# Attention as a rotation lane and a score lane with banks of their own, rotation from PSUM, one global projection run, head products in two column halves

## What is computed

```python
x = L0_attn_x                       # (16, 512, 128)
xn = _layernorm(x)
s = _L0_attn_ref(xn, ...)           # gated linear recurrence ("gru"), 256 states
g = _silu(_L0_ffn_ref(xn, ...))     # two layers: windowed attention + gated MLP
x = x + s * g
xn = _layernorm(x)
s = _L1_attn_ref(xn, ...)           # softmax attention, 16 heads ("glob")
g = _silu(_L1_ffn_ref(xn, ...))     # 8 experts, top 2
x = x + s * g

# one layer of _L0_ffn_ref
q, k, v = split(shift_token(x) @ wqkv, 3)          # 8 heads of 64
q, k = rotary_xpos(l2norm(q) * qs, l2norm(k) * ksc)
x = x + local_attention(q, k, v) @ wo              # windows of 64 and the one before
h = layernorm(shift_token(x)) @ w1 + b1
x = x + (a * gelu(g)) @ w2 + b2                    # a, g = split(h, 2)

# _L1_attn_ref
sim = einsum('bnkh,bmhk->bnhm', q, k)              # keys of 16, values of 64
attn = softmax(sim * scale, axis=1)                # over n
o = einsum('bnhm,bmhv->bnhv', attn, v)
return einsum('bnhv,dhv->bnd', o, output_proj)
```

## Time and profile before

| | |
|---|---|
| median of 3 runs | 4378.24 us (4377.39 to 4380.41) |
| span of the profiled execution | 4382.6 us |
| PE, PE weight load | 3673.3 us (84%), 1761.1 us (40%) |
| DVE, ACT, POOL | 2821.0 (64%), 2427.6 (55%), 999.9 us (23%) |
| global head products, PE (o_bank) | 2048 passes, 1008.9 us |
| DMA | 124.19 MB, 28 GB/s |

### The profile page before, as it was taken

The page is one execution under the profiler, slowest core; times in us unless marked ns, Lnnn a source line. Parts: engine busy times, 40 slices in busy tenths (PEclk is TensorE's granted clock), DMA queues, the critical chain, the costliest instruction groups (busy, mean ns, idle before and its releaser), DMA issues.

```text
span 4382.6 us, 66677 instructions
## 1 busy us (share of the span) xinstructions
PE 3673.3 (84%) x19970; PEld 1761.1 (40%) x20144; DVE 2821.0 (64%) x4828; ACT 2427.6 (55%) x5081; POOL 999.9 (23%) x719
## 2 busy tenths in 40 slices
PE   4678798898988889898888889898888989898876
PEld 3445343444443344444344444444434444343321
DVE  3562676667676766767676676767667676767432
ACT  2343565565656566565656656565655656565432
POOL 1210222112222221222222221223221122222110
PEclk7689899999999999999999999999999999999987
DMA  2002001010000101010010101000010100001010
GB/s 60 1 3 75 8 18 43 18 47 15 32 27 15 46 16 45 19 43 12 15 46 19 43 18 44 18 23 32 18 43 18 47 15 30 29 12 46 15 49 13
DMA packets 112589, 124.19 MB, mean 28 GB/s; under 512 B 12434, under 2 KB 85692, under 8 KB 112188
## 3 DMA queue, kind: packets, MB, share of 16 engines
q1 hardware_dynamic: 112124, 119.26, 8.4%
q0 software_dynamic: 64, 0.01, 0.0%
HBM read 64.70 MB, written 54.53 MB: 27 GB/s over the span
## 4 chain that ended last, share of the span: by engine, by line
PE 50%; issue 22%; DVE 17%; ACT 5%; POOL 5%; DVEq 1%; SPq 1%; DMA 0%; POOLq 0%; ACTq 0%
PE pb L569 23%; PE o_bank L569 14%; PE s L569 4%; PE pb L695 3%; PE y_bank L569 2%; PE pb L664 2%; DVE nmax L1284 2%; POOL scratch L1369 2%; POOL scratch L1364 2%; DVE stat L1178 1%; POOL vsc L1402 1%; DVE stat L1199 1%; DVE scratch L1191 1%; ACT ex L1016 1%; PE pb L719 1%
## 5 line engine op out<-in xcount | busy, mean ns | idle before, releaser
L1284 DVE TENSOR_REDUCE nmax<-s 128x1 f32<-128x512 f32 x1024 | 687.3, 683 | 693.2 <-PE s L569 689.7
L569 PE MATMUL o_bank<-ex,vsc 128*64 128x512 f32 x2048 | 1008.9, 639 | 34.9 <-POOL vsc L1402 33.0
L1016 ACT ACTIVATE ex<-s,nmax 128x512 f32<-128x512 f32 x1024 | 697.7, 685 | 556.0 <-DVE nmax L1284 508.7
L1402 POOL TENSOR_TENSOR vsc<-vrow,rinv 128x256 f32<-128x256 f32 x256 | 189.5, 740 | 1964.2 <-DVE rinv L1292 1961.6
L569 PEld LDWEIGHTS o_bank<-ex,vsc 128*64 128x64 f32 x2048 | 279.0, 147 | 666.2 <-issue 594.1
L1364 POOL TENSOR_TENSOR scratch<-scratch 128x1024 f32<-128x1024 f32 x128 | 314.0, 2453 | 776.9 <-DVE scratch L1191 641.5
L569 PE MATMUL s<-qs,ks 96*128 96x512 bf16 x1024 | 365.7, 392 | 102.8 <-ACT ex L1016 92.7
L569 PE MATMUL pb<-wqkv,hsh 128*128 128x512 f32 x768 | 390.0, 644 | 47.0 <-DVE hsh L1171 41.8
L569 PE MATMUL pb<-kT,qT 64*64 64x64 f32 (+1 forms) x6144 | 325.7, 254 | 37.3 <-issue 16.4
L664 PE MATMUL pb<-const,scratch 128*128 128x128 f32 x1024 | 184.9, 340 | 198.7 <-POOL scratch L1369 196.8
L1369 POOL TENSOR_TENSOR scratch<-scratch,stat 128x1024 f32<-128x1024 f32 x128 | 255.8, 1999 | 266.5 <-DVE stat L1203 266.1
(11 more groups left out here) (193 smaller groups left out, 6190.7 us busy)
## 6 DMA issues: line engine op xcount, KB each, us to landing
parts_store<-side SPq DMA_DIRECT2D x64, 384.0 KB, 2.6
qs<-parts_store SPq DMA_DIRECT2D x128, 192.0 KB, 2.7
ks<-parts_store SPq DMA_DIRECT2D x128, 192.0 KB, 3.1
parts_store<-side SPq DMA_DIRECT2D x64, 256.0 KB, 2.8
parts_store<-side SPq DMA_DIRECT2D x64, 128.0 KB, 2.7
xin<-in_L_attn_x SPq DMA_DIRECT2D x16, 256.0 KB, 4.2
ex<-in_L_ffn_w SPq DMA_DIRECT2D x16, 256.0 KB, 3.1
out<-yrow SPq DMA_DIRECT2D x16, 256.0 KB, 3.6
```

The source lines that it names most:

```text
L569: return pe.matmul(o, l, r, start=start, stop=stop, skip_group_check=True)
L1016: A(ex[:, h % 2, m, :], s_bank[c % 2][:], ACT.Exp, bias=nmax[:, c % 8:c % 8 + 1], accum_out=rsum[:, h % 2, m:m + 1]).then_inc(GA, 1)
L1284: V.tensor_reduce(nmax[:, c % 8:c % 8 + 1], s_bank[c % 2][:], X, ALU.max, negate=True).then_inc(GV, 1)
L1402: G.tensor_tensor(vsc[:, h % 2], vrow[:, :, V1 * h:V1 * h + V1], rinv[:, h % 2, :].unsqueeze(2).broadcast_to([P, 4, V1]), ALU.mult).then_i ...
```

## The change

Four things, and a new written order for every engine:

- attn is split into "qkv" (q, k, v, rotation, tq, tk) and "attn" (score to wo), which run as two lanes, "p" (qkv0, qkv1) and "r" (attn0, post0, attn1). The rotation lane uses banks a and b; q's and k's products stay there until DVE has multiplied them. Scores use bank c, and a new bank e (its place comes from y_bank) holds pturn, pv, oturn and wo in turn.
- ACT squares q and k with one instruction of 1024 columns and no longer copies them; DVE's rotation reads PSUM.
- "sim" and "av" take a pair of heads at a time: a step w holds two blocks m of both heads, and its four av matmuls go to the halves of o_bank in turn. The sums of a pair close after two steps.
- proj is one run of eight matmuls into o_bank after the last head, reading a larger o1T; the following "store" uses o_bank too.

The two loads of the experts' routing move from POOL's queue to SP's.

```diff
+def qkv_steps():
+    s = [("shift",)]
+    for t in range(NT):
+        s += [("q", t), ("k", t), ("rot", t)]
+        if t:
+            s += [("tq", t - 1), ("tk", t - 1)]
+        s += [("v", t), ("vb", t), ("rot2", t)]
+    return s + [("tq", NT - 1), ("tk", NT - 1)]
...
 def attn_steps():
+    s, units = [], 2 * NT
+    for u in range(units + 2):
         if u < units:
+            s += [("score", u), ("prob", u)]
         if 1 <= u <= units:
+            s += [("pturn", u - 1), ("pv", u - 1)]
+        if u >= 2 and u % 2 == 0:
+            s += [("oturn", u // 2 - 1), ("wo", u // 2 - 1)]
...
-        "a": lane("attn0", 0, STEPS["attn0"]) + lane("post0", 0, STEPS["post0"]) + lane("attn1", 0, STEPS["attn1"]),
+        "p": lane("qkv0", 0, STEPS["qkv0"]) + lane("qkv1", 0, STEPS["qkv1"]),
+        "r": lane("attn0", 0, STEPS["attn0"]) + lane("post0", 0, STEPS["post0"]) + lane("attn1", 0, STEPS["attn1"]),
...
+                    mm((bank_a, bank_b, bank_a)[n], hsh[:, P * t:P * t + P], wqkv[:, l, INNER * n:INNER * (n + 1)])\
...
+                    if u and u % 2 == 0:
+                        need(pe, f, "dve", b, ("wo", u // 2 - 1), "x")
+                    elif u:
+                        need(pe, f, "dve", b, ("pv", u - 1), "o")
                     need(pe, f, "act", b, ("prob", u), "p")
                     for r in range(PAIRS):
-                        last = pe.transpose(bank_b[:, P * r:P * r + P], prob[u % 2][:, r, :], ident)
+                        last = pe.transpose(bank_e[:, P * r:P * r + P], prob[u % 2][:, r, :], ident)
...
-                    for m in range(4):
-                        last = mm(o_bank[V1 * (h % 2):V1 * (h % 2) + V1, :], vsc[:, h % 2, m, :], ex[:, h % 2, m, :],
-                                  start=(m == 0), stop=(m == 3))
+                    for j in range(4):
+                        last = mm(o_bank[V1 * (j % 2):V1 * (j % 2) + V1, :], vsc[:, w % 2, j, :], ex[:, w % 2, j, :],
+                                  start=(w % 2 == 0 and j < 2), stop=(w % 2 == 1 and j >= 2))
...
-                    mm(y_bank[:], wo1[:, p, :], o1T[:], start=(p == 0), stop=(p == 7)).then_inc(GE, 1)
+                    need(pe, glob, "act", b, ("o", H1 // 2 - 1), "t")
+                    for p in range(H1 // 2):
+                        last = mm(o_bank[:], wo1[:, p, :], o1T[:, p, :], start=(p == 0), stop=(p == H1 // 2 - 1))
+                    last.then_inc(GE, 1)
...
-                    A(l_sq[:, INNER * k:INNER * (k + 1)], src, ACT.Square).then_inc(FA, 1)
...
-                    A(l_qk[t % 2][:, INNER * k:INNER * (k + 1)], src, ACT.Copy).then_inc(FA, 1)
+                    A(l_sq.rearrange("p (k n) -> p k n", k=2), pb[:, 0:2, :], ACT.Square).then_inc(FA, 1)
...
-                    src = l_qk[t % 2].rearrange("p (k h d) -> p k h d", k=2, d=DH)
+                    src = pb[:, 0:2, :].rearrange("p k (h d) -> p k h d", d=DH)
```

More of the change, by code:

```diff
@@ L134, in glob_steps @@
     s = []
-    for h in range(H1 + 1):
-        for m in range(4):
[L137 to L145, removed]
+    for w in range(H1 + 1):
+        for j in range(4):
+            if w < H1:
+                s += [("sim", w, j)]
+            if w and j == 0:
+                s += [("scale_v", w - 1)]
+            if w and j == 1:
+                s += [("av", w - 1)]
+            if w and w % 2 == 0:
+                p = w // 2 - 1
+                s += {2: [("o", p)]}.get(j, [])
     half = s.index(("sim", H1 // 2, 0))
     values = [("values", n) for n in range(2 * NT)]
-    return values, s[:half], s[half:] + [("gate",), ("store",)]
+    return values, s[:half], s[half:] + [("proj",), ("gate",), ("store",)]
 NORM_MARKS = {
@@ L666, in attn_does @@
                     last.then_inc(f.sem["pe"], 1)
[L667 removed]
+            def attn_does(l, b, s):
+                f, kind = attn[l], s[0]
+                if kind == "score":
                     t, par = s[1] // 2, s[1] % 2
@@ L735, in post_does @@
                         if l == 0:
-                            need(pe, attn[0], "dve", b, ("score", 2 * NT - 1), "sub")
+                            pass
                         elif isinstance(b, int) and b == B - 1:
@@ L820, in glob_does @@
                     for t in range(NT):
-                        last = pe.transpose(y_bank[:, P * t:P * t + P], yf[:, P * t:P * t + P], ident)
+                        last = pe.transpose(o_bank[:, P * t:P * t + P], yf[:, P * t:P * t + P], ident)
                     last.then_inc(GE, 1)
@@ L847, in expert @@
                 for t in range(NT):
-                    last = pe.transpose(y_bank[:, P * t:P * t + P], eacc[:, t, :], ident)
+                    last = pe.transpose(o_bank[:, P * t:P * t + P], eacc[:, t, :], ident)
                 last.then_inc(expert_pe, 1)
@@ L1320, in expert @@
                 dve.wait_ge(expert_pe, 8 * E + 1)
-                V.tensor_scalar(es[0], y_bank[:], bias1, None, ALU.add).then_inc(expert_dve, 1)
+                V.tensor_scalar(es[0], o_bank[:], bias1, None, ALU.add).then_inc(expert_dve, 1)
                 dve.wait_ge(expert_dve, n + 1)
```

346 lines of the change are left out of this document (162 added, 184 removed).

## The result

The changed kernel takes 4136.8 us (median of 4 runs, 4116.0 to 4152.2) against 4379.3 us beside it: a ratio of 0.944, 95% interval 0.941 to 0.947. Forecast were 3785 us, 3600 to 4010. The direction was right, the size was not: 5.6% instead of 13.6%.

The account below looks back on a forecast made before the run. One attention lane (about 249 of 252 us) bounds the kernel, PE (220) close behind. Parts of 100, 24, 90 and 4 make a 218 us period: 442 us saved over 13 iterations, 158 outside; 3785 us, range 3600 to 4010.

Parts of the forecast that it names:

- Column halves: Global lane's head products: two passes run in the time of one, a step takes 1.87 us, 1.7 less.
- the 2.3 us: Head-product step if matmuls start and end strictly in order: 2.3 us for 1.87, a total near 3835.
- the halves don't overlap: Rival, chance 0.11: head products' halves don't overlap at 512 columns; period 235, 3950 to 4200 us.
- It is no longer the limit; the engines are: Attention lane: split in two it needs 53 us a layer, 134 us an iteration, far below 252; engines limit instead.
- the ring: Theory of the experiments, not forecast: score, max, subtract, exp, copy, value products, next score follow one another, 6.0 us a unit.
- new waits: Rival, chance 0.09: new bank waits in score and rotation lanes, 41 and 30 us, eat all; 4390 to 4600.
- Layer 1 at 90 us, DVE its limit: Steady layer 1: DVE takes over as limit with 81.4 us of work, at density 0.90, so 90 us.
- PE's 72.5 us in layer 1 and 187 in all: PE's work per iteration after the change: 72.5 us in layer 1, from 87.4, and 187 in all.
- Layer 0: Steady layer 0: PE's work falls from 110.0 to 94.7 us, at density 0.95, so 100 us.
- MLP 0 and turn: Between the layers and at the iteration's end: MLP 0 stays at 24 us, the turn at 4.
- Outside the loop: First iteration 50 us less, second and first after the loop 30 and 33, end phase 45: together 158.
- The projection: One run of 16 passes in layer 0: 7.0 us on PE, +0.8, then PE waits some 1 to 2 us.

Follow-up runs that it names:

- x1: The kernel before with only the two column halves of o_bank, lanes, banks, order and spread projection as they were: 4155.9 us, 0.949.
- x3: The changed kernel with ACT's copy of the turned probabilities of unit u-1 moved ahead of the exp of unit u: 3978.7 us, 0.909.
- x7: The changed kernel with the global lane's maxima on DVE taken over 256 of the 512 columns: 4083.7 us, 0.932.
- x13: The changed kernel with six of a head pair's eight products into o_bank cut to 64 columns: 4130.3 us, 0.943.
- x5: The kernel of x3 with the projection's run, and its gate on DVE, moved behind the last tile's wo of layer 0: 4033.3 us, 0.921.
- x12: The kernel of x3 with the projection cut into two runs of four products, around the last tile's wo of layer 0: 3985.9 us, 0.909.
- x9: The kernel of x3 with the copies of the turned q and k ahead of the next tile's Ln on ACT: 3971.2 us, 0.907.
- x14: The kernel of x3 with the same head products cut to 64 columns as in x13: 3988.3 us, 0.911.
- x15: The kernel of x3 with the added score products of x11: 4121.9 us, 0.942.
- x6: The kernel of x3 with the next unit's score put ahead of the turn of the output rows on PE: 4221.7 us, 0.962.
- x4: The changed kernel with unit u-1's turn ahead of unit u's score on PE, and its copy ahead of u's exp on ACT: 4550.6 us, 1.040.
- x11: The changed kernel with two of four global-lane score products of each step made three times over: 4199.2 us, 0.958.

## Why the prediction was wrong

- **Column halves: right.** 1.94 us a step for a forecast 1.87, and nearly the whole gain (x1). The strict program order of the Trainium skill ("TensorE: Matmul & The Clock Gate", "Part 3: Packing small matmuls — row/col tiling") is not refuted by this; what the 1.94 us refute is the 2.3 us that I had worked out from it for matmuls of two passes. The measured 4136.8 us lie in the range of the rival "the halves don't overlap" (3950 to 4200), but by chance: its mechanism did not happen.
- **"It is no longer the limit; the engines are": this step failed.** I had the rotation lane at 9.5 us a tile, two last units at 15, 53 us a layer. In the first iteration, with nothing beside it, a layer takes 103.5 and 95.3 us, where I had 65 for the first at its cold clock; the walk of layer 0, MLP 0 and layer 1, for which I had 130, takes 225 us there (48.9 to 274.2). Two things were mis-sized. The rotation: v's copies are 13 to 18 us apart there. The tile's 9.5 us were summed at full clock; with the matmuls of q, k, v and the turns at half clock the same sum comes to some 13 us (an estimate: they double, 3.5 us more). And the score lane was priced as if only its last two units were left behind the rotation, 15 us. When the last v is copied (102.53), PE is only about to make the scores of the fourth unit (103.99), so that five are left; the layer ends at 152.4, 50 us later. In x3 the same stretch takes 36 us (102.34 to 138.4): the ring is 14 of the 35 us too many, the other 21 are there without it.

```profile
102.53 0.69 DVE L1173 COPY va<-pb 128x512 f32<-128x512 f32 x1 [2.91 <-PE pb L576]
...
103.99 0.63 PE L576 MATMUL pb<-masks,identb 128*128 128x512 bf16 x1
```

  This is near the rival "new waits", which I gave 0.09 and which has these waits but not their outcome, slower than before: I counted its copy and norm, 0.85 us a unit, and called a unit's own scores "PE work ahead of the next turn". They are PE work, but through ACT's order the copy waits for them as well. The lists in the diff show it: "prob" of u stands ahead of "pturn" of u-1 on ACT, where the kernel before gave the value products one more unit of distance.
- **Layer 1 at 90 us, DVE its limit: failed.** 103.2, DVE 0.74 busy. x3 takes 6 us off it with DVE unchanged; x7 takes a tenth of DVE's work away for 1.7 us a period. That leaves 7 us of layer 1 to which no run gives a cause.
- **PE's 72.5 us in layer 1 and 187 in all: mis-sized.** 84.7 and 198.3 measured (the four windows). I subtracted work at the clock of before, 0.92; it is 0.83 now. That relief of PE alone lowers the clock, and part of the saving comes back, x13 shows by itself.
- **Layer 0: right** (100 for 103.3; PE 94.7 for 92.4), MLP 0 and turn too.
- **Outside the loop: 50 us for 158.** The first two iterations were to save 80 and save nothing. For the first one's 50 the ring is part of the cause: x3 gets 21 of them back (15 + 6); the rest stays in x3 too. Behind the loop the saving is some 55 for a forecast 78. In the end phase (group of PE in the last 150 us) a head pass has a mean of 1052 ns, for 689 over the whole run: the granted clock is 0.69 there, and a step of 8 passes takes 3.6 us (57.6 / 16), the half-clock price.

```profile
L576 PE MATMUL o_bank<-ex,vsc 128*64 128x512 f32 x128 | 57.6, 1052 | 15.6 <-POOL vsc L1404 12.9 <-ACT ex L1012 2.7
```

- **The projection** as one run stands 7 us in the score lane's way in layer 0. I had the 7 us as PE's work and a wait of 1 to 2 behind it, but nothing for the lane that stands still meanwhile; x5 and x12 show that moving it only moves the wait.

What stays open: 10 of the 18.7 us that separate 236.7 from the forecast 218. x3, x9 and x12 all have a period of 228.2 to 228.5 though their layers differ. x14 and x15 show that it is not PE's work alone, x9 and x12 that it is neither the rotation's order on ACT nor the run's place. That several circles through PE's one written order are closed at once, and PE's clock falls when one opens, fits these, but no run shows it. The loads of x, taken one by one, hold a sign of something else: from the second on, every period of x3, x9 and x12 lies between 228.4 and 228.9 us; from the fourth on, every one of x1 and x13, two kernels with little in common, between 238.8 and 239.1; those of the changed kernel go from 234.6 to 242.9. So kernels whose work differs keep the same period to half a us. Rings alone give no reason for that. A period that falls into step with the rises and falls of PE's clock might, but this is a guess that no run here tests; until it is settled, that x12's 3.8 us came to nothing doesn't prove that another circle took them.

## What to carry to other kernels

Splitting work into lanes gives each a queue of its own only in the plan: every engine still has one written order. Follow one unit round all engines in that order and see whether its copy stands behind another unit's wait. Here one moved step on ACT was worth 158 us, two thirds of what the whole change gave, and the version with it (x3, and x9 at 3971 us) beats both kernels. But such a look finds a candidate and not its price: of the moves tried (x3 to x6, x9, x12) x3 alone paid clearly, and x4, which looks much like it, cost 414 us. When an engine is relieved, price the rest of its work at the clock that its new rests will bring, not at the old one. And run the cheap half of a change alone first: x1 is one small edit and holds nine tenths of the gain.

## What the runs showed of the hardware

- Two fp32 products of 512 columns in the two column halves run in nearly the time of one: 8 passes in 1.94 us for 3.58.
- PE with most of 2048 head passes cut to 64 columns: no gain, the granted clock 0.840 for 0.878, and untouched 512-column passes longer (q, k, v 811 for 729 ns, scores 453 for 421).
- The reverse: 1024 passes added in x11 raise the clock from 0.878 to 0.909; the kernel pays 62 us for about 218 us of added work at full clock (an estimate: 1024 times 0.21 us, since two such passes in a row take 0.60 us and one 0.38 to 0.39). PE's busy time rises by 78 us only.
- One ACT Square over two PSUM banks (1024 columns) takes 1.02 us, DVE's product of 1024 columns from PSUM 1.22 us against 1.34 from SBUF (groups of the changed kernel):

```profile
L1181 DVE TENSOR_TENSOR scratch<-pb,tab 128x1024 f32<-128x1024 f32 x128 | 155.7, 1217 | 25.8 <-ACT scratch L922 22.8
L922 ACT ACTIVATE scratch<-pb 128x1024 f32<-128x1024 f32 x128 | 130.3, 1018 | 189.9 <-PE pb L576 189.1
```
